# First-layer routing moved into the attention pairs of a two-layer attention and mixture-of-experts kernel

## What is computed

```python
xn = _layernorm(x)
x = x + _L0_attn_ref(xn, ...) + _L0_ffn_ref(xn, ...)
xn = _layernorm(x)
x = x + _L1_attn_ref(xn, ...) + _L1_ffn_ref(xn, ...)
```

## Time and profile before

| What | us |
|---|---|
| median of 3 runs (3389.18 to 3394.2) | 3392.34 |
| the profiled execution's own time | 3389.78 |
| its span, first to last instruction | 3387.8 |
| TensorE, VectorE, ScalarE, GpSimd busy | 2885.2, 2168.9, 1646.0, 1430.5 |

### The profile page before, as it was taken

The page is one execution under the profiler, slowest core; times in us unless marked ns, Lnnn a source line. Parts: engine busy times, 40 slices in busy tenths (PEclk is TensorE's granted clock), DMA queues, the critical chain, the costliest instruction groups (busy, mean ns, idle before and its releaser), DMA issues. The chain is left out here.

```text
span 3387.8 us, 61538 instructions
## 1 busy us (share of the span) xinstructions
PE 2885.2 (85%) x21526; PEld 2314.3 (68%) x21526; DVE 2168.9 (64%) x6229; ACT 1646.0 (49%) x3452; POOL 1430.5 (42%) x2033
## 2 busy tenths in 40 slices
PE   4414989989898998987898888899889999999986
PEld 3313777777787887774666666666578888888864
DVE  4543776777767676775777777776654445454576
ACT  1201444544444454454666666666445455555554
POOL 3753332424333242437665666532312222222277
PEclk9997999999999999998999999999999999999999
DMA  8852565665656566531233333321065555555455
GB/s 272 300 215 107 209 258 196 237 235 219 225 219 256 199 238 238 219 118 30 51 91 91 102 99 101 95 87 62 33 226 194 208 205 215 204 219 200 157 100 120
DMA packets 192070, 580.15 MB, mean 171 GB/s; under 512 B 22856, under 2 KB 144656, under 8 KB 157456
## 3 DMA queue, kind: packets, MB, share of 16 engines
q1 hardware_dynamic: 154896, 525.03, 42.3%
q0 software_dynamic: 36864, 51.14, 7.4%
HBM read 450.14 MB, written 125.96 MB: 170 GB/s over the span
## 5 line engine op out<-in xcount | busy, mean ns | idle before, releaser
L1241 POOL TENSOR_TENSOR al<-t,ah 128x512 fp32r<-128x512 f32 x220 | 288.3, 1310 | 1080.8 <-ACT ah L1418 1078.6
L818 PE MATMUL bank<-masks_bf,ident_bf 128*128 128x128 bf16 (+1 forms) x2304 | 578.2, 251 | 82.4 <-ACT ksT L1500 41.2
L772 PE MATMUL bank<-xh,gu 128*128 128x256 f32 x3520 | 630.9, 288 | 11.2 <-DVE t L1683 2.4
L1832 DVE TENSOR_REDUCE st<-bank 128x1 f32<-128x512 f32 (+3 forms) x1024 | 424.0, 481 | 238.2 <-PE bank L825 238.0
L1513 ACT ACTIVATE pt<-bank 128x512 f32<-128x512 f32 (+1 forms) x1152 | 513.2, 539 | 39.3 <-PE bank L828 38.0
L772 PEld LDWEIGHTS bank<-xh,gu 128*128 128x128 f32 x3520 | 506.7, 193 | 33.1 <-issue 21.6
L818 PEld LDWEIGHTS bank<-masks_bf,ident_bf 128*128 128x128 bf16 x2304 | 224.7, 98 | 345.0 <-issue 73.3
L828 PE MATMUL bank<-qaT,ksT 128*128 128x512 f32 (+3 forms) x1536 | 434.6, 391 | 0.0
L825 PE MATMUL bank<-ksT,qsT 128*128 128x512 f32 (+3 forms) x1536 | 431.8, 379 | 0.0
L772 PE MATMUL bank<-xl,gu 128*128 128x256 f32 x1760 | 355.2, 284 | 0.0
L1521 ACT ACTIVATE oT<-bank 128x512 f32<-128x512 f32 x192 | 114.3, 596 | 495.5 <-PE bank L895 495.5
(11 more groups left out here) (249 smaller groups left out, 5333.9 us busy)
## 6 DMA issues: line engine op xcount, KB each, us to landing
gu<-wu_scratch SPq DMA_DIRECT2D x110, 2056.0 KB, 7.9
dn<-wd_scratch SPq DMA_DIRECT2D x110, 1024.0 KB, 9.4
xs<-xs_scratch SPq DMA_DIRECT2D x110, 264.0 KB, 8.9
ys_scratch<-yb SPq DMA_DIRECT2D x110, 256.0 KB, 9.7
raw<-in_gu SPq DMA_DIRECT2D x16, 1024.0 KB, 10.1
wu_scratch<-hi SPq DMA_DIRECT2D x16, 1024.0 KB, 5.4
wu_scratch<-lo SPq DMA_DIRECT2D x16, 1024.0 KB, 4.0
xs_scratch<-empty SPq DMA_DIRECT2D x32, 264.0 KB, 2.8
```

Source lines behind the costliest of these rows:

```text
L772: mm = pe.matmul(bank[:, TS * h:TS * (h + 1)], gu[:, col:col + P], x[s % 2][:, TS * k:TS * (k + 1)], start=(n == 0), stop=(n == len(terms) ...
L818: pe.matmul(bank[:, diag:diag + P * len(unit)], ident_bf[:, :], masks_bf[:, 0 if which == "q" else 1, 0:len(unit), :].rearrange("p n k -> ...
L1241: pool.tensor_tensor(em["al"][s % 2][:, m, :], em["t"][g % 2][:, :], em["ah"][s % 2][:, m, :].bitcast(F32), ALU.subtract).then_inc(al_read ...
L1832: ins = dve.reduce_max(st[:, 0, r:r + 1], bank[:, first:first + width], AX.X)
```

## The change

`route_first` and `tabulate` go. `setup`, `load` and the loads of `fold` become one block, which no longer loads x. The routing of batch b stands in pairs 2b - 3 to 2b + 4 of the attention, on each engine at a fixed place of `pair_alone`; expert e's weights are split by ScalarE at the end of pair 2e and by VectorE at the end of pair 2e + 1, with one `raw` buffer instead of two. GpSimd's scatters of batch b stand in pairs 2b + 3 and 2b + 4, eight in each. VectorE makes the tile table in pair 17 and compacts the slots in pair 19. SyncE clears the ends of the experts' lists, waits for scatters and weights and loads the first two tiles in pair 18. The pieces of the first layer's tiles stand in pairs 20 to 48, fifteen to a pair, so 2, 3, 2, 3, 2, 3 in the slots; pair 48 has the last six. The banks of the X ring serve the routing too.

```diff
-PIECES = (9, 6)
-SPANS = tuple((a, a - -6 * t // n) for a, t, n in zip((0, 138), TILES, PIECES))
+PIECES = (15, 6)
+SPANS = tuple((a, a - -6 * t // n) for a, t, n in zip((20, 138), TILES, PIECES))
...
+        scatter_at = {2 * b + 3 + half: [(b, half)] for b in range(B) for half in range(2)} if em else {}
+        def routes(G, lag):
+            b, odd = divmod(G - lag, 2)
+            return em is not None and odd == 0 and 0 <= b < B
...
@@ TensorE, pair_alone
+                    if routes(G, 0):
+                        turn_routed(G // 2)
+                    if routes(G, 3):
+                        turn_combine((G - 3) // 2)
...
+                    if routes(G, 2):
+                        route_ranks((G - 2) // 2)
+                    if routes(G, 1):
+                        route_logits((G - 1) // 2)
+                    if routes(G, 3):
+                        route_bias((G - 3) // 2)
...
@@ SyncE
+                    if routes(G, 1):
+                        e = (G - 1) // 2
+                        if e + 1 < E:
+                            load_raw(e + 1)
+                        store_raw(e)
...
+                    if em and G == begins[0] - 2:
+                        clear_ends(0)
+                        routed()
+                        first_tiles(0)
...
@@ GpSimd, after stack(G + 2) and head_rms
+                    if routes(G, -2) and G // 2 + 1 >= 2:
+                        route_std(G // 2 + 1)
+                    for b, half in scatter_at.get(G, ()):
+                        route_scatter(b, half)
...
@@ ScalarE, pair_alone
+                    if routes(G, 0):
+                        take_routed(G // 2)
+                    if routes(G, 3):
+                        take_combine((G - 3) // 2)
+                    if routes(G, 2):
+                        route_exponents((G - 2) // 2)
...
+                    if routes(G, 0):
+                        first_high(G // 2)
...
@@ VectorE, pair_alone, after normalize
+                    if routes(G, 2):
+                        route_weigh((G - 2) // 2)
...
@@ after heads_out and context_out
+                    if routes(G, 2):
+                        route_place((G - 2) // 2)
+                    if routes(G, 1):
+                        route_select((G - 1) // 2)
+                    if routes(G, 3):
+                        add_bias((G - 3) // 2)
+                    if routes(G, -1):
+                        route_rows((G + 1) // 2)
+                    if routes(G, -3) and (G + 3) // 2 >= 2:
+                        route_stats((G + 3) // 2)
...
@@ after norm_heads
+                    if routes(G, 1):
+                        first_low((G - 1) // 2)
+                    if em and G == begins[0] - 3:
+                        first_table()
+                    if em and G == begins[0] - 1:
+                        first_compact()
```

More of the change, by code:

```diff
@@ L208, in sem_maker, with setup @@
         return new, done
-    def setup():
+    def setup(masks, pairs, fills):
         new, done = sem_maker()
[L213 to L240, removed]
@@ L243, in fold @@
-    def fold(weights):
-        new, done = sem_maker()
[L245 to L293, removed]
@@ new lines, in setup, with _ @@
+        loaded, cast, filled = new("loaded"), new("cast"), new("filled")
+        pairs = [(to[tuple(slice(None) for _ in to.shape)], dram[name]) for to, name in (
+            (ident, "c_ident"), (masks, "c_masks"), (tie, "c_tie"), (upper, "c_upper"), (pick, "c_pick"),
+            (first, "c_first"), (running, "c_first"), (steps, "c_steps"), (count, "c_count"))] + pairs
+        with nc.Block() as block:
+            @block.sync
+            def _(sp):
+                for to, frm in pairs:
+                    sp.dma_start(to, frm).then_inc(loaded, 16)
+                sp.wait_ge(loaded, 16 * len(pairs))
+            @block.vector
+            def _(dve):
+                for i in range(2):
+                    dve.memset(V[i][:, :, :, HD:HD + 1], 1.0).then_inc(filled, 1)
+                dve.memset(flag[:, :], 0.0).then_inc(filled, 1)
+                dve.memset(minus_half[:, :], -0.5).then_inc(filled, 1)
+                dve.memset(ones[:, :], 1.0).then_inc(filled, 1)
+                for to, value in fills:
+                    dve.memset(to, value).then_inc(filled, 1)
+                dve.wait_ge(loaded, 16 * len(pairs))
+                dve.tensor_copy(ident_bf[:, :], ident[:, :]).then_inc(cast, 1)
+                dve.tensor_copy(masks_bf[:, :, :, :], bcast(masks[:, :, :], 2, 2)).then_inc(cast, 1)
+                dve.wait_ge(cast, 2)
+                dve.wait_ge(filled, 5 + len(fills))
@@ new lines, in route_rows @@
+                def route_rows(b):
+                    small = ro["stats"][b % 2]
+                    dve.wait_ge(r_std, b + 1)
+                    if b >= 4:
+                        dve.wait_ge(scattered[b % 4], per_batch * (b // 4))
+                    for t in range(NT):
+                        dve.tensor_scalar(ro["rows"][b % 4][:, t, 0:D], acc[:, NT * b + t, :], small[:, 8 + 2 * t:9 + 2 * t],
+                                          small[:, 4 + t:5 + t], ALU.subtract, ALU.mult).then_inc(r_rows, 1)
@@ new lines, in route_weigh, with route_place @@
+                def route_weigh(b):
+                    dve.wait_ge(r_exp, b + 1)
+                    weigh(dve, chain, r_comb)
+                    dve.wait_ge(r_comb, b + 1)
+                    dve.tensor_scalar(ro["rows"][b % 4][:, :, D:XR], rt[:, 6, :].rearrange("p (t e) -> p t e", e=E), 0.5, None,
+                                      ALU.mult).then_inc(r_w, 1)
+                def route_place(b):
+                    dve.wait_ge(x_full, X.full(f"Rk{b}"))
+                    place(dve, chain, X.bank(f"Rk{b}"), ro["big"], CHOICES[0], slots[0][:, NT * b:NT * (b + 1), :],
+                          (x_dve, X.count[f"Rk{b}"]), r_slot)
@@ L2111, in _ @@
                 shift(0)
+                if em:
+                    route_rows(0)
                 if kinds[0] == "mla":
```

469 lines of the change are left out of this document (227 added, 242 removed).

## The result

The changed kernel takes 3412.85 us, the median of five runs (3407.2 to 3418.41), against 3389.26 us for the kernel before, the median of its five. The ratio is 1.0074, with a 95% interval of 1.005 to 1.0098: slower by 0.7%, where I forecast 3350 us, faster by 1.2%. The time lies 7 us inside the upper edge of my range (3265 to 3420), on the side to which I gave 0.20. Two more series of the changed kernel gave 1.0064 (1.005 to 1.0077) and 1.0085 (1.0062 to 1.0108).

A forecast was written before the change was run, and what follows sets the result against it. Expert pairs were taken as bound by TensorE, after a serial routing front. Pair 48's copy at 1465, plus 15 and 1865, gave a 3345 us span, 3350 us measured time against 3392.3; range 3265 to 3420.

The forecast's parts named there:

- the side to which I gave 0.20: Whole kernel: the change makes it slower than 3399 us, chance 0.20.
- the term of the sum for an expert pair: Pairs with fifteen pieces: 24.7 now, 8.9 for one more tile, 2.8 gate wait, less 0.2, giving 36.2 us each.
- the new wait: Slot 4 of 28 expert pairs: TensorE waits 2.8 us for VectorE's clip of the previous gate.
- The pipeline starts at 22 us: Front: without the serial routing the pipeline's first load is issued at 22 us, against 266.5.
- Routing pairs 19 us each: Pairs 3 to 18 with routing inside: 19 us each, floor 16.5, ceiling 22.
- The last scatter at 421: End of the routing pairs: GpSimd issues its last scatter at 73 + 44 + 304 = 421 us.
- the rival by which VectorE would stretch the scatters: Routing pairs: each scatter waits for one VectorE operation, 0.3 us, 40 us in all; 3390 us, chance 0.05.
- The change of stage: Between last scatter and pair 20's experts: waiting for scatters and loading first weights takes 15 us, experts starting at 436.
- the clock rival: Expert pairs: clock falls at every gate wait, 3.4 us each, 95 us in 28; 3445 us, chance 0.12.
- No gate wait: Expert pairs: the clip is in time or the wait replaces another, 79 us not lost; 3270 us, chance 0.13.
- Nothing hidden: Pairs 0 to 19: none of the routing is covered, 432 instead of 363 us; 3419 us, chance 0.08.
- GpSimd's floor: Routing pairs: they reach GpSimd's own work, 16.5 us a pair; 3310 us, chance 0.12.

The follow-up runs named there:

- experiment 2: Changed kernel with 22 useless matmuls filling TensorE's wait for the gate in each first-layer expert pair: 3343.35 us, ratio 0.9863 to the kernel before.
- experiment 1: Changed kernel with VectorE's maxima of the next pair split in two halves around slot 3's expert work: 3276.8 us, ratio 0.9665 to the kernel before.
- experiment 4: Changed kernel with the high and low parts of the routing's weight split swapped between odd and even pairs: 3390.55 us, ratio 1.0015 to the kernel before.
- 8: Changed kernel unaltered 3421.68 us, with maxima split 3317.61, with stores of low parts and blank blocks written one pair later 3416.12, with both edits 3316.99.
- experiments 1 to 3: Changed kernel with, separately, maxima split (3276.8 us), the gate's wait filled with useless matmuls (3343.35), and the attention's output matmuls moved ahead of slot 4 (3323.88).
- serial_front: Kernel before, routing still ahead of the attention, but expert tiles in pairs 20 to 48, fifteen pieces each: 3499.29 us, ratio 1.0323 to the kernel before.
- the first group: The first four follow-up kernels, run on one chip in turns with the kernel before (3389.1 us); its split kernel took 3276.8 us.

## Why the prediction was wrong

**The step that failed** is the term of the sum for an expert pair: "24.7 + 8.9 + 2.8 - 0.2 = 36.2 us". It has the new wait, at the right place and of the right length, and leaves out what the clock does behind it. I had that as a rival with 0.12, argued away because "that fall lies between transposes on both sides, the new wait between full matmuls". The trace and experiment 2 show that this is no protection: with full matmuls on both sides, 2.75 us of idleness brought the clock from 2.4 to 1.2 GHz. Per fall I had 3.4 us; it is 1.5 us (4.4 against 2.9 us for the two pieces), since the clock is back at 1012.35, and as a mean over the pairs it is 1.15 (experiment 2) to 1.47 us (experiment 1). A pair measured 37.76: 1.56 us above the term, 42 us in 27 pairs. The prediction says that the rival decides from 1.5 us a pair on; so the clock, 31 to 40 of these 42 us, took nearly all of the gain away, and a second, smaller miss made it a loss. The Trainium skill, TensorE: Matmul & The Clock Gate, "Why this matters for your kernels", says that idle gaps between bursts cost the clock; the trace agrees, with 0.62 behind the wait, and with 0.98 instead of 0.94 over the stage when the gap is filled. The page warns of gaps a little longer than these; here 2.65 to 2.84 us were enough, at 25 of 27.

**The sum, term by term**, forecast against measured. The pipeline starts at 22 us: 21.88, the row of SyncE's first load, against the earlier trace rows.

```profile
21.88 0.39 SPq L873 DMA_DIRECT2D xb<-in_x  x1
```

Routing pairs 19 us each, from pair 3 on: 19.1 over pairs 0 to 15. The last scatter at 421: at 439.6. They did not lengthen: the 128 take 136.4 us, 1.07 each, against 1.09 in the earlier trace rows. In this row, which gives the least, median and largest in ns, and the first and last start, the median is 963 ns; it is 963 in the kernel before too:

```profile
L1237 POOL DMA_INDIRECT xs_scratch<-rows,slots x128: 959/963/1967, 138.7 to 439.6; - x128
```

So the rival by which VectorE would stretch the scatters is out. The Trainium skill, SBUF — State Buffer, "Who interferes with whom", has VectorE and GpSimd block each other only where both need the port pair that they share, which not every instruction of VectorE does; the prediction left that condition out. No run here shows such a wait of the scatters. Of the 19 us, 3 are the first copy (97.9 against 95), 9 the first three pairs (18.3, 15.6 and 19.2 against 44 in all), the rest the pairs after them, at a clock of 0.77 where I had read 0.89 from the gather pairs. Neither experiment 4 nor 8 settles what sets these pairs. The kernels of experiments 1 to 3 had the copy of pair 16 at 376 to 378 us, some 26 earlier, which no reason of mine foresaw; so some 26 us of this stretch go with the stalls, whose cause is open. The change of stage took 452.2 - 439.6 = 13 us where I had 15; the experts begin at 452.2 instead of 436, after a wait for the first weights:

```profile
452.24 0.79 PE L525 MATMUL bank<-xh,gu 128*128 128x256 f32 x2 [2.83 <-DMA gu<-wu_scratch]
```

Pair 48 took 20.1 us against 22, and 3411.1 - 1542.0 = 1869 us follow the copy of pair 49 against 1865.

**The balance.** 66 us too low in the span: some 20 by the start of the experts and the stage before it, 42 by the 27 expert pairs, the rest small. With 36.2 us a pair the span would be 3369, and the kernel faster than before. With the routing on time but 37.76 a pair it would be 3391, no change. The sign went by both, the larger part being the clock. That the total lies inside my range is luck: the range was meant to leave the clock rival out, and had that rival's price been my 3.4 us a pair, it would lie outside.

**The other rivals.** "No gate wait" names a state that the order of VectorE forbids; experiment 1 makes it, and gives 104 us, not 79, because the clock comes with it. "Nothing hidden" is out: `serial_front` needs 86 us more to pair 20. "GpSimd's floor" was not reached in the changed kernel; in the split kernel of the first group the 16 routing pairs took 376.0 - 98.1 = 278 us, 17.4 each, close to it.

**A version that beats both.** The changed kernel with the maxima split: 0.9665 and 0.9784 of the kernel before in two groups of runs, 104 us under the changed kernel beside it.

## What to carry to other kernels

When pieces of work are packed denser between the instructions of an in-order engine, look at which piece comes to stand first behind the long block of the engine that serves it: here a gate whose bank comes free only behind four maxima and a shift, where a down piece used to stand. Price such a wait twice, once as idle time and once as what TensorE's clock loses behind it; at 2.8 us the second was half as much again, at 1.6 us nothing, and waits of 2.1 us had it at 13 of 28. And look in the trace whether an edit of a queue did what it was written for: moving a store to a later place in the program moved it by at most some 1.5 us, since its engine had nothing to wait for in between. Two probes tell the idle time and the clock apart cheaply: fill the wait with useless matmuls (the clock alone comes back), and move the serving instruction forward (both come back).

## What the runs showed that I had not expected

Useless work made the kernel 31 us faster in its expert pairs: 22 matmuls more in each, 36.61 instead of 37.76 us a pair, clock 0.98 instead of 0.94. And one and the same kernel took 3276.8 and 3317.6 us in two series, each within 0.4%, while the kernel before, run in between, took 3389 in both. The difference lies in the stretch where ScalarE, VectorE, GpSimd and TensorE all run the routing and the attention at once, 36 of 41 us by pair 16, and goes with stalls of 1 to 5 us that the profile ascribes to nothing that fits: TensorE has none there in the faster series and 10 in the slower.
